# A kernel of gated attention and experts: attention of one row placed between the experts of the row before, V products in one piece, and all rows written out

## What is computed

```
xn = layernorm(x)
# causal attention, 16 heads of 8
energy = (where(causal, -10000, q k^T scale) - threshold) / tau
attn   = 1 - tanh(energy)**2 ; attn /= sum(attn) + 1e-6
s      = (attn v) Wo^T
# softmax attention on h = rmsnorm(xn), 16 heads of 8
X  = xn + softmax(q k^T scale) v wo
h2 = rmsnorm(X)
combine = top 2 of 8 of softmax(h2 router), renormed
moe = swiglu_shared(h2) + sum_e combine[e] * swiglu_e(h2)      # F = 256
out = x + s * silu(X + moe)
```

## Time and profile before

| | us |
|---|---|
| median of 3 runs (lowest, highest) | 1255.82 (1254.42, 1259.35) |
| the profiled execution, its time | 1256.73 |
| its span, first to last instruction | 1255.0 |
| TensorE busy | 1120.9 |
| VectorE busy | 840.3 |
| ScalarE busy | 649.3 |
| GpSimd busy | 338.4 |
| mean granted clock of TensorE | 0.946 |

### The profile page before, as it was taken

One profiled execution on the slowest core, in us unless ns is written; L12 is line 12 of the kernel. 1 busy time (PEld: TensorE's weight loads), 2 busy tenths in 40 slices (PEclk: granted clock), 3 DMA queues, 4 the chain that ended last, 5 costly groups with the idle time before them and its releaser, 6 DMA issues.

```text
span 1255.0 us, 21105 instructions
## 1 busy us (share of the span) xinstructions
PE 1120.9 (89%) x7112; PEld 480.4 (38%) x7112; DVE 840.3 (67%) x1692; ACT 649.3 (52%) x873; POOL 338.4 (27%) x177
## 2 busy tenths in 40 slices
PE   2479999899998899899998999989999899998998
PEld 1112454234541354314543245422464234542365
DVE  6365976569657686576865688655976558656673
ACT  4039821597117861278513883149721597218841
POOL 5400443015420334103341035310543014420013
PEclk8559999799998999989998999989999799999999
DMA  5520432003411135102341033410342104400020
GB/s 173 99 35 2 77 103 42 28 2 77 118 26 28 24 55 134 22 17 44 70 107 28 2 63 99 58 28 2 77 109 35 29 4 74 130 15 18 1 69 8
DMA packets 67970, 66.86 MB, mean 53 GB/s; under 512 B 7760, under 2 KB 59216, under 8 KB 67728
## 3 DMA queue, kind: packets, MB, share of 16 engines
q1 hardware_dynamic: 65088, 61.26, 22.9%
q10 hardware_dynamic: 2768, 4.06, 0.9%
HBM read 50.22 MB, written 14.81 MB: 52 GB/s over the span
## 4 chain that ended last, share of the span: by engine, by line
PE 65%; issue 10%; ACT 10%; DVE 9%; DMA 3%; SPq 2%; POOL 1%; ACTq 1%; DVEq 0%; POOLq 0%
PE M L906 12%; PE O L980 10%; PE O L964 10%; PE S L996 8%; PE S L998 5%; PE S L997 5%; PE S L939 4%; ACT PT L525 4%; DVE PT L676 4%; DVE nmax L639 3%; PE M L1069 1%; SPq L321 1%; PE M L899 1%; PE M L893 1%; PE M L918 1%
## 5 line engine op out<-in xcount | busy, mean ns | idle before, releaser
L525 ACT ACTIVATE PT<-S 128x1024 f32<-128x1024 f32 (+1 forms) x448 | 421.1, 973 | 122.7 <-PE S L939 119.6
L639 DVE TENSOR_REDUCE nmax<-M 128x1 f32<-128x512 f32 x512 | 338.3, 688 | 200.1 <-PE M L906 196.6
L676 DVE SCALAR_TENSOR_TENSOR PT<-PT 128x768 f32<-128x768 f32 (+1 forms) x192 | 215.7, 1173 | 95.9 <-ACT PT L525 95.6
L906 PE MATMUL M<-stackK,stackQ 48*128 48x512 bf16 x512 | 214.5, 434 | 60.9 <-DMA stackK<-scrK 27.5
L964 PE MATMUL O<-PT,V 128*12 128x256 f32 (+3 forms) x2816 | 250.7, 437 | 0.0
L559 ACT ACTIVATE PT<-S 128x1024 f32<-128x1024 f32 x72 | 73.9, 1026 | 313.0 <-PE S L998 313.0
L400 POOL TENSOR_TENSOR split<-split,parts 128x512 f32<-128x512 f32 x32 | 93.1, 2909 | 489.3 <-ACT parts L486 489.3
L415 POOL TENSOR_TENSOR PT<-PT,CB 128x1024 f32<-128x1024 f32 x56 | 132.8, 2373 | 336.3 <-DMA CB<-scrC 171.1
L939 PE MATMUL S<-stackQ,stackK 64*128 64x512 bf16 (+3 forms) x1024 | 205.6, 362 | 18.8 <-DMA stackQ<-mTZ 9.3
L906 PEld LDWEIGHTS M<-stackK,stackQ 48*128 48x128 bf16 x512 | 46.9, 95 | 299.3 <-issue 175.6
L980 PE MATMUL O<-PT,wdn 128*128 128x512 f32 x288 | 151.5, 625 | 0.0
(11 more groups left out here) (174 smaller groups left out, 932.7 us busy)
## 6 DMA issues: line engine op xcount, KB each, us to landing
CB<-scrC SPq DMA_DIRECT2D x64, 256.0 KB, 5.4
stackQ<-scrQ SPq DMA_DIRECT2D x192, 64.0 KB
stackK<-scrK SPq DMA_DIRECT2D x192, 64.0 KB
scrQ<-parts SPq DMA_DIRECT2D x16, 384.0 KB, 4.5
scrK<-parts SPq DMA_DIRECT2D x16, 384.0 KB, 8.3
PT<-in_w_gu ACTq DMA_DIRECT2D x2, 1152.0 KB, 8.2
xin<-in_x SPq DMA_DIRECT2D x8, 256.0 KB, 2.9
xres<-in_x SPq DMA_DIRECT2D x8, 256.0 KB, 3.3
```

The costliest lines, as they stand in the source:

```text
L525: a.activation(PT[:, n % SLOTS, 2 * q * w:2 * q * w + 2 * w].rearrange("p (r n) -> p r n", r=2), S[k][:, :].rearrange("p (r n) -> p r n", ...
L639: v.tensor_reduce(nmax[:, h % 2, h // 2, t:t + 1], M[k][:, :], AX.X, ALU.max, negate=True).then_inc(m_read[k], 1)
L676: v.scalar_tensor_tensor(p, p, 1.0, p, ALU.subtract, ALU.mult).then_inc(weighed, 1)
L906: t_.matmul(M[k][:, :], stack["Q2"][a:a + ROW_ADD, hp, t * 128:t * 128 + 128], stack["K2"][a:a + ROW_ADD, hp, :], start=True, stop=True).t ...
```

## The change

The rows are no longer a loop: a Python loop over b from -1 to 8 writes all of them out, for every engine. The list ITEMS gives the order in one body: units 0 to 15 of row b, experts 0 to 4 of row b-1, units 16 to 19 of row b, experts 5 to 8 of row b-1, units 20 to 23 of row b, G (the gate of row b-1), units 24 to 27 of row b. BEHIND says which V product (V) or down product (D) stands at the end of an item. In b = -1 only the small works for row 0 are done, in b = 0 no experts, in b = 8 nothing but experts and the end of row 7. Further:

- `with_v` takes all 512 columns at once; before, 12 of the 16 softmax units did it in two halves, one behind each half of the scores.
- Run X of the maxima has 24 and no longer 32; 8 form a run W, found in units 0 and 1 and needed by unit 4.
- xnT to K2 of the next row stand in units 12 to 14, V1 and the causal result (oT1, ctxT1, proj1) of the row before in units 10 to 14.
- The norms' last step (8 TENSOR_SCALARs of 128x128), the second norm's, the rest of h2, and the gated product move from VectorE to GpSimd; combT's copy moves to ScalarE; expert 8's weighing moves from VectorE to GpSimd; the copy of xn to x1 on GpSimd is gone. xn, x1, h2hi, h2lo are double.
- CB holds three experts' weights and no longer eight; AB and CB have memory of their own (EX), apart from PT.
- SP issues the loads of Q1 and K1 at a body's start, and run W's rows behind them.

```diff
-RUNS = {"X": (0, 4), "Y": (4, 6), "Z": (6, 8)}
+RUNS = {"X": (0, 3), "W": (3, 4), "Y": (4, 6), "Z": (6, 8)}
+ITEMS = ([("U", n) for n in range(N1)]
+         + [("E", e) for e in range(5)] + [("U", N1 + u) for u in range(4)]
+         + [("E", e) for e in range(5, NE)] + [("U", N1 + u) for u in range(4, 8)] + [("G", 0)]
+         + [("U", N1 + u) for u in range(8, 12)])
...
+place("U", 12, 1, 1, "xnT")
+place("U", 14, 1, 1, "K2")
+place_maxima("X", 1, [("E", 3, 1, 2), ("E", 4, 1, 2), ("U", 16, 1, 1), ("U", 17, 1, 1), ("U", 18, 1, 1), ("U", 19, 1, 1),
...
@@ sync @@
+            for b in range(-1, B + 1):
...
+                        scores_done(b - 1, UNITS - 1)
+                    for name in ("Q1", "K1"):
+                        load_stack(b, name)
+                    maxima_rows(b, "W")
+                if b >= 1:
+                    spread_weights(b - 1)
+                if 0 <= b < B:
+                    maxima_rows(b, "Y")
+                    maxima_rows(b, "Z")
+                if b < B - 1:
+                    for name in ("Q2", "K2"):
+                        store_parts(b + 1, name)
...
+                        scores_done(b, N1 - 1)
+                    for name in ("Q2", "K2"):
+                        load_stack(b + 1, name)
...
@@ gpsimd @@
+            for b in range(-1, B + 1):
+                if b < B - 1:
+                    norm_apply(b + 1)
+                    split_steps(b + 1, "Q2")
+                    split_steps(b + 1, "K2")
+                if b >= 1:
+                    for e in range(1, 5):
+                        weigh_expert(b - 1, e)
+                if 0 <= b < B:
+                    second_norm(b)
...
@@ vector @@
+                    if item == ("U", 10) and b < B - 1:
+                        norm_stats(b + 1)
...
@@ tensor @@
-                    i0, i1 = (128 * j if n >= N1 else 0, L) if half is None else (half * L // 2, (half + 1) * L // 2)
+                    i0 = 128 * j if n >= N1 else 0
...
-            with pe.Fori(0, B - 1) as it:
-                row(LOOP.row(it), it, True)
-            row(LAST, B - 1, False)
+                    for i in range(3):
+                        if i < 2 and kind == "U" and 0 <= b < B:
+                            scores(b, n, i)
+                        elif i < 2 and kind == "E" and b >= 1:
+                            half_expert(b - 1, n, i)
+                        elif i == 2 and item in BEHIND:
+                            what, m = BEHIND[item]
+                            r = b - 1 if what == "D" or item in (("U", 0), ("U", 1)) else b
+                            if 0 <= r < B:
+                                (second_product if what == "D" else with_v)(r, m)
+                        for r, name in works(b, item, i):
+                            work(r, name)
```

More of the change, by code:

```diff
@@ L72 @@
-PLACES[9] += ["maxT_Z"]
-PLACES[16] += ["xnT", "hT"]
-PLACES[17] += ["Q2"]
-PLACES[18] += ["K2"]
-PLACES[19] += ["V2", ("oT2", 0)]
-PLACES[20] += [("oT2", 1), ("oT2", 2)]
-PLACES[21] += [("oT2", 3)]
-PLACES[22] += ["ctxT2"]
-PLACES[23] += ["proj2"]
-PLACES[25] += ["Q1"]
-PLACES[26] += ["h2T"]
-PLACES[27] += ["logits", "K1"]
-PLACES[EXPERT] += ["suffix"]
-PLACES[EXPERT + 1] += [("oT1", 0), "combT", ("oT1", 1)]
-PLACES[EXPERT + 3] += [("oT1", 2), ("oT1", 3)]
-spread(MAX["X"], {EXPERT + e: n for e, n in enumerate((0, 0, 5, 4, 4, 5, 6, 6, 2))})
@@ L119, with four @@
-FIRST = Uses(False, True)
-LOOP = Uses(True, True, FIRST.total)
-LAST = Uses(True, False, LOOP.row(B - 1).before)
-S_USES = UNITS + NE
-O_USES = (2 * NG // 2 + 1, 2 * NG // 2)
-WEIGHED = 2 * len(STAGE2)
-DOWNS = NE + 1
-DEPTH = 3
-DVE_FIRST, DVE_ROW = 39, 55
-SPLIT_STEPS = 8
+    assert at == len(MAX[run])
+def four(*units):
+    return [("U", n, i, count) for n in units for i, count in ((0, 1), (1, 1), (2, 2))]
+place_maxima("W", 0, four(0, 1))
+place("U", 2, 0, 0, "maxT_W")
+place_maxima("Y", 0, four(2, 3, 4, 5))
@@ new lines @@
+place("U", 6, 0, 0, "maxT_Y")
+place_maxima("Z", 0, four(6, 7, 8, 9))
+place("U", 10, 0, 0, "maxT_Z")
+place("U", 10, 1, -1, ("oT1", 0))
+place("U", 10, 2, -1, ("oT1", 1))
+place("U", 11, 1, -1, ("oT1", 2))
+place("U", 11, 2, -1, ("oT1", 3))
+place("U", 12, 0, 0, "V1")
+place("U", 12, 1, 1, "xnT")
+place("U", 12, 2, 1, "hT")
+place("U", 13, 1, 1, "Q2")
+place("U", 13, 2, -1, "ctxT1")
+place("U", 14, 1, 1, "K2")
+place("U", 14, 2, -1, "proj1")
+place("E", 2, 0, 1, "V2")
+place("E", 2, 2, 0, ("oT2", 0), ("oT2", 1))
@@ L1065, in work @@
                 elif name == "suffix":
[L1066 removed]
+                    pe.wait_ge(*read(r, "V1"))
+                    k = begin(r, name)
                     for t in range(NT):
```

1102 lines of the change are left out of this document (524 added, 578 removed), and 4 rows, old and new, of the table BEHIND.

## The result

The changed kernel takes 1482.86 us (median of 4 runs, 1475.1 to 1495.3), the kernel before beside it 1255.12 (1253.66 to 1259.35): ratio 1.182, 95% interval 1.173 to 1.191. It is 228 us slower. I had forecast 85 us. Medians here are over all executions of a kernel; a ratio, its interval and every difference between two kernels go by the executions within 1.5% of its fastest, whose median, up to 13 us lower, is given as "for differences" where it is another.

The account below looks back on a forecast made before the run. TensorE, busy 89% of the span, was taken as the bound, with VectorE or ScalarE pacing softmax units. Terms 73 + 130.5 + 6 x 157 + 132.5 + 60 = 1338, plus 1.7, gave 1340 us; range 1235 to 1392.

Parts of the forecast that it names:

- W's wait: At unit 4: W lands some 20 us after loads begin, wanted at 17.5 (some 4 of start); 2.5 us.
- Units 0 to 9: Softmax units, run W adding 8 maxima: 40 maxima at 0.82 us each, 33 us a full body.
- VectorE near 90%: Sign expected in units 0 to 9: 3.3 us each, VectorE near 90% busy, TensorE lower than before.
- Stack K2: Run X's first maximum, expert 3: TensorE stands still 4 us, then low clock costs 3 us, in a full body.
- Experts 5 to 8: Experts with two down products, 16 maxima, h2T, logits, suffix and two V products: 25.5 us a full body.
- Body 0: Attention alone: W late by 9 us, 22 us for stack K2's loads with no experts covering them; 130.5 us.
- Written-out rows: At the loop's end: 3.30 us gap and slow clock behind it go; perhaps 5 us a row, no separate term.
- V in one piece: Twelve softmax units: saves at most 2.3 us of TensorE, but VectorE idles 0.35 us; both inside other terms.
- Norms on GpSimd at nothing: Norm's eight TENSOR_SCALARs on GpSimd: between nothing and twice 2.3 us; taken as nothing, xnT standing two units behind.
- The first: Rival: loads overlap, W and K2 are in time, full body 147.5 us, total 1264 (1235 to 1290); chance 0.16.
- The second: Rival: experts keep TensorE full, bodies 135 or 140 us, total 1182 or 1212; against it, buffer depth; chance 0.13.
- The third: Rival: several low-clock stretches or GpSimd late (sign: TENSOR_SCALAR above 1 us); 10 us a body more, 1400; chance 0.09.

Follow-up runs that it names:

- ninth experiment: Changed kernel with 36 extra matmuls ahead of the wait for stacks Q2 and K2 in bodies 1 to 6; 1469.28 us.
- second kernel: Changed kernel with run X's 24 maxima beginning in unit 16, no longer in expert 3; 1406.06 us.
- seventh: Changed kernel with run X from unit 16, loads of Q1 and K1 behind rows of W, Y, Z, and those runs' turns one step later; 1351.85 us.
- tenth kernel: The seventh, with wgu_lo formed on VectorE behind unit 15 of body 0, no longer on GpSimd in the preparation; 1342.54 us.
- first and third experiment: First: changed kernel, W's rows issued ahead of the loads of Q1 and K1, 1483.18 us; third: that plus run X from unit 16, 1432.92 us.
- sixth: The second kernel with the loads of Q1 and K1 behind the rows of W, Y and Z on SP; 1347.84 us.

## Why the prediction was wrong in size

Direction and the two waits were right, and each was seen in the unit and expert named. A body came out at 172.3 us and not 157, body 0 at 171.8 and not 130.5. Of the 146 us between the forecast span (1338) and the measured one (1483.8), the preparation has 3, body 0 41, the six full bodies 92, body 7 19, and the end gives 9 back.

The step that failed is the pricing of the waits and of what stands behind them: W's wait was mis-sized (2.5, measured 6.5 a body), so was K2's (4, measured 7.9), and the low clock behind W's wait and in body 0, and the longer experts 5 to 8 behind K2's, were put at nothing. Stage by stage, the mean over bodies 2 to 6 against the forecast:

| stage | forecast | measured |
|---|---|---|
| units 0 to 9 and the wait for W | 35.5 | 40.8 |
| units 10 to 15 | 22 | 22.5 |
| experts 0 to 4, wait for K2, low clock | 35 | 38.3 |
| units 16 to 19 | 11.5 | 10.7 |
| experts 5 to 8 | 25.5 | 31.6 |
| units 20 to 27 | 27.5 | 27.4 |

*Units 0 to 9.* The term of 33 us was right: clean, they take 32.0, with the new run in them. The wait for W was mis-sized: 51.8 / 8 = 6.5 us a body and not 2.5. The loads were not slower than taken (in body 4 the scores that need W's rows start 16.9 us after the first issue of a load, I had some 20). What failed is the "some 4 of start": unit 4 was ready 12.6 us after the body's start in body 4 (777.58), not 17.5. And I put no low clock behind this wait; in body 4 the stage has 0.83, and takes 8.0 us more than clean, 4.84 of them the wait. My sign "VectorE near 90%" was off too: clean it is busy 25.7 of 32.0 us, 80%.

*Stack K2.* "4 us of TensorE standing still" measured 47.1 / 6 = 7.9: the loads took some 24 and not 20 us from issue to use. The low clock behind it, which I had at 3, is worth 2.3 by the ninth experiment.

*Experts 5 to 8* were the largest miss within a body, 6 us. In the second kernel the same 16 maxima stand in them and they take 27.6 us; so some 4 us come of what the K2 wait, or the four maxima that it holds up, upsets ahead of them. The low clock behind it is not the reason: in the ninth, with that clock full and the wait still there, they take 30.8. In body 4 of the changed kernel GpSimd was busy 14.1 us there and in the clean body of the seventh 10.4, the weighing being late; which link carries it was not tried.

*Body 0* was the largest miss of one body, 41 us. Its stages are units 0 to 9, units 10 to 15 with the wait for stack K2, units 16 to 19 with sixteen maxima of empty experts, and units 20 to 27:

```profile
75.87:129.84 53.97, 34.76 (x147) 5.07 (x148) 34.17 (x42) 22.59 (x25) 15.56 (x8) 0.59 0.23 49
129.84:186.23 56.39, 25.03 (x153) 10.42 (x150) 9.76 (x38) 17.97 (x25) 12.88 (x14) 0.77 0.26 43
186.23:223.66 37.43, 28.42 (x133) 11.55 (x132) 23.72 (x44) 11.20 (x20) 6.82 (x5) 0.61 0.00 0
223.66:247.68 24.02, 19.84 (x166) 7.45 (x165) 23.14 (x45) 17.01 (x27) 9.64 (x6) 0.86 0.15 45
```

I had 42, 40, 23.5 and 25. The wait for K2 came as forecast (21.3, I had 22), that for W was shorter (4.4, I had 9). What failed is that I costed the body at full clock, and it has 0.69; and that I hadn't seen the wait of 9.9 us for mhW beside GpSimd's long instruction.

*Body 7* has a wait for W of 10.0 us and takes 44.4 us in units 0 to 9 (I had 35.5), and 33.9 in units 20 to 27 (I had 24.5); why the second is so long was not looked into.

*Written-out rows*: 2.4 us a row and not 5, since only the gap went and the low clock stayed. *V in one piece*: I noted the 0.35 us of idle VectorE and left it inside other terms; alone it costs 3.5 us a row (28 / 8), the reverse of TensorE's 2.3 us saved. *Norms on GpSimd at nothing*: right but for the preparation, where TensorE waits 12.5 us for xn and before waited 9.9; moving them back costs 20 us or more, by the very route that I described for the statistics (the oT1 blocks behind them).

*Rivals.* The first falls: the loads do not overlap so far that anything is in time. The second ("TensorE is kept full") needs its reason against it named better: not the depth of the buffers but VectorE's reductions, which the experts don't cover as long as they stand in blocks of their own; with three quarters of each reduction taken away, bodies of 142 us are there, no better than the old row with the same and without its gap. The third, several waits and stretches of low clock, is what happened; 1400 was still too little. Its sign on GpSimd came half: the TENSOR_SCALARs of the second norm take 1.40 us, those of the first 0.8. Break-even at 143 us a body was too generous: with 416 us outside the six bodies, as in the tenth kernel, it is (1255 - 416) / 6 = 140.

## What to carry to other kernels

A load in a queue served in order delays everything issued behind it, and most of all where the issuing engine waits for a small store behind the load before it goes on; moving one victim ahead makes the next the victim (first and third experiment), moving the load behind all that is urgent frees them nearly all (sixth). When experts' work is placed between stages, ask which engine paces the stages that lose their cover: here 32 maxima stood beside matmul-bound experts for next to nothing (with short reductions that stage fell from 68.4 to 67.9 us), and the eight of run W now stand beside VectorE-bound units at full price. And count what fills and drains the pipeline first: 64 us over eight rows had to be earned at some 11 a body before anything was won.
